# A vision tower on one core: halves of the gate, adjacent logits and moved statistics in the image loop; residual on TensorE in the last part

## What is computed

```python
h = patches(x) @ W.T                               # 768 -> 192
q, k, v = silu(h @ Wq), silu(h @ Wk), silu(h @ Wv) # 12 heads of 16
a = ((q @ k.T) * causal_decay) @ v                 # per head
a = (a * sigmoid(h @ Wg1 @ Wg2)) @ Wo
h = T(h + layernorm(a) * ln_w + ln_b)
# soft mixture: 64 slots, each an expert of its own
xn = rms_norm(h) * norm_w
logits = l2(slots) * scale @ l2(xn).T              # 64 x 196 an image
y = softmax_over_tokens(logits) @ xn               # a slot's input
y = gelu(y @ fc1[s] + b1[s]) @ fc2[s] + b2[s]      # for each slot s
out = T(h + softmax_over_slots(logits).T @ y)
```

## Time and profile before

| | us |
|---|---|
| median of 3 runs (1191.71 to 1193.66) | 1193.31 |
| profiled execution, its own time | 1190.01 |
| its span | 1188.3 |

### The profile page before, as it was taken

How to read it: one execution, slowest core, us unless ns; L and a number is a source line. 1 busy time by engine, 2 the same in 40 slices (tenths; PEclk the granted TensorE clock), 3 DMA queues, 4 the chain that set the end, 5 groups by cost and what they waited for, 6 DMA issues and landing times.

```text
span 1188.3 us, 35236 instructions
## 1 busy us (share of the span) xinstructions
PE 1076.5 (91%) x13008; PEld 837.5 (70%) x13008; DVE 862.8 (73%) x2154; ACT 738.8 (62%) x1711; POOL 628.2 (53%) x967
## 2 busy tenths in 40 slices
PE   7799999999999999999999999999988999996653
PEld 6677788777777777877777778777765655554331
DVE  5878888888888888888888888888872222223996
ACT  6357777777777777777777777777753111110666
POOL 4556666666666665666666666566641000001664
PEclk9999999999999999999999999999999999998555
DMA  4511222111111122111111112211074999995885
GB/s 157 201 52 53 65 88 66 54 54 54 54 54 54 54 69 83 64 54 54 54 54 54 54 54 79 76 61 54 14 306 129 420 423 423 423 424 166 246 257 177
...
## 3 DMA queue, kind: packets, MB, share of 16 engines
...
## 4 chain that ended last, share of the span: by engine, by line
POOL 36%; issue 27%; PE 22%; DVE 10%; ACT 2%; DVEq 1%; DMA 1%; POOLq 1%; ACTq 0%; SPq 0%
POOL xl L440 14%; PE ps L1463 6%; POOL xn L526 5%; PE ps L1482 4%; POOL ra L517 4%; POOL hTl L496 4%; POOL rstd L507 2%; DVE res L1103 2%; POOL invn L500 2%; PE ps L1498 2%; DVE st L1109 2%; PE ps L1489 2%; POOL qd L477 1%; DVE p_sb L947 1%; PE ps L1227 1%
## 5 line engine op out<-in xcount | busy, mean ns | idle before, releaser
L947 DVE TENSOR_TENSOR p_sb<-ps,dec 98x1568 f32<-98x1568 f32 x96 | 171.6, 1788 | 64.2 <-PE ps L1227 64.1
L440 POOL TENSOR_TENSOR xl<-x_sb,xh 128x392 fp32r<-128x392 f32 x186 | 190.2, 1049 | 45.7 <-ACT xh L597 45.7
L496 POOL TENSOR_TENSOR hTl<-hT,hTh 128x392 fp32r<-128x392 f32 x64 | 66.3, 1035 | 146.3 <-ACT hTh L705 98.6
L763 ACT ACTIVATE hg<-ps 128x768 f32<-128x768 f32 x32 | 25.9, 810 | 144.3 <-PE ps L1489 144.3
L883 DVE SCALAR_TENSOR_TENSOR t<-t,rstd,hb 98x192 f32<-98x192 f32 x128 | 93.1, 767 | 15.9 <-POOL rstd L507 15.5
L1095 DVE COPY y2st<-ps 128x192 f32<-128x192 f32 x32 | 11.4, 357 | 120.5 <-PE ps L1463 120.5
L554 POOL CAST pickb<-pick 128x128 fp32r (+1 forms) x32 | 9.4, 293 | 150.4 <-PE ps L1489 150.4
L780 ACT ACTIVATE o_sb<-res,nb,rstd 98x192 f32<-98x192 f32 x128 | 59.6, 536 | 44.6 <-DVE nb L1118 44.0
L1260 PE MATMUL ps<-p_sb,vpad 98*32 98x98 f32 x3072 | 85.7, 252 | 1.5 <-DVE p_sb L947 1.5
L1260 PEld LDWEIGHTS ps<-p_sb,vpad 98*32 98x32 f32 x3072 | 64.7, 110 | 26.7 <-issue 26.7
L1513 PE MATMUL ps<-y2b,cbuf 64*98 64x192 f32 x256 | 49.4, 537 | 37.6 <-POOL y2b L567 37.6
...
## 6 DMA issues: line engine op xcount, KB each, us to landing
...
```

What stands on the lines that cost most here:

```text
L440: pool.tensor_tensor(xl[:, k], x_sb[:, k], xh[:, k].bitcast(F32), ALU.subtract)\
L496: pool.tensor_tensor(hTl[:, k], hT[:, k], hTh[:, k].bitcast(F32), ALU.subtract).then_inc(hTl_rdy[k], 1)
L947: dve.tensor_tensor(dst, src, rate.unsqueeze(2).to_broadcast([T, 4, 2, TOK]), ALU.mult)\
```

## The change

1. **Gate in halves.** `gate(i, 0)` stays; `gate(i, 1)`, with the wait for ScalarE's copies of bank 1, comes after scores part 2.
2. **Logits adjacent.** The four products of the logits of a pair's two images stand together, alternating between the images, before scores part 2.
3. **ScalarE in the step** rounds `x` and copies the logits before the second half of the gate.
4. **VectorE in the step** takes `residual_statistics(i - 1, 1)` after `kts`.
5. **Drain**: half of `xn` and of `hb` is scaled on ScalarE; the squares of pair 31 come before the logits of pair 30 are copied; several steps change place; fewer `idle_products`.
6. **Two-row runs.** `h2` is stored as token rows (two DMAs a pair, 768 B runs); a partition of the last part holds two rows that follow each other, so that `h2r` and the output move in runs of 1536 B. The weights `cbuf` are then read with stride 2.
7. **Last part.** TensorE multiplies `h2r` with the identity into the banks (two products of 384 columns) and adds the four products to it; a signal is sent for each bank. VectorE takes statistics straight from PSUM and adds the bias; GpSimd makes `negm` and `nb3`; ScalarE scales from PSUM; SP issues the stores.

```diff
@@ sync
+                for a in range(2):
+                    sp.dma_start(h2_dram[j, a].rearrange("(k p) d -> p k d", k=2), h2[:, 2 * a:2 * a + 2, :])\
+                        .then_inc(h2_stored, 16)
...
-            sp.wait_ge(sc_mm, 3 * NP)
+            sp.wait_ge(g_mm, 2 * NP)
             load_weights(2, 2)
...
+            def refill(p, n):
+                sp.wait_ge(cmb_mm, 2 * p + 2)
+                load_comb(p + DEEP, n)
+                load_h2(p + DEEP, n)
+
+            def store_out(p, n):
+                sp.wait_ge(o_rdy, 4 * p + 4)
+                sp.dma_start(out_v[p], o_sb[:, n].rearrange("m (a k) d -> m a (k d)", a=2)).then_inc(out_stored[n], 16)
...
+                    refill(p, n)
+                    store_out(p - 2, (n - 2) % DEEP)
@@ gpsimd
+                pool.tensor_tensor(negm[:, n], mv3[:, n, :, 0], expo[0:T, 2], ALU.mult).then_inc(negm_rdy, 1)
                 pool.wait_ge(ve4_rdy, p + 1)
                 pool.tensor_tensor(rstd3[:, n], ve[0:T, n], expo[0:T, 0], ALU.pow).then_inc(rstd3_rdy, 1)
-            def bias(p, n):
-                pool.tensor_tensor(y2b[:, n], y2r[:, p], b2[:, :], ALU.add).then_inc(y2b_rdy, 1)
+                pool.wait_ge(negm_rdy, p + 1)
+                pool.wait_ge(rstd3_rdy, p + 1)
+                pool.tensor_tensor(nb3[:, n], negm[:, n], rstd3[:, n], ALU.mult).then_inc(nb3_rdy, 1)
@@ scalar
                 act.activation(gt[:, 0:PT], ps[:, 0, 0:PT], ACT.Tanh, scale=0.5).then_inc(g_sb, 1)
+                if more:
+                    round_x(i + 1, 1)
+                if d:
+                    logits_kept(i - 2)
                 act.wait_ge(g_mm, 2 * i + 2)
...
-                if more:
-                    round_x(i + 1, 1)
...
+            for t in range(2, 4):
+                act.activation(xn[0:T, t], gn[0:T, t], ACT.Copy, scale=cosc[:, t:t + 1]).then_inc(xn_rdy, 1)
             token_rows(one)
+            squares(last)
             logits_kept(one)
             slot_exponentials(one)
             token_exponentials(one)
-            squares(last)
+            for t in range(2, 4):
+                act.activation(hb[0:T, t], gn[0:T, t], ACT.Copy, scale=cosc[:, t:t + 1]).then_inc(xn_rdy, 1)
...
-                    act.activation(o_sb[:, n, t], res[:, n, t], ACT.Identity,
+                    act.activation(o_sb[:, n, t], ps[0:T, 2 * n + t // 2, (t % 2) * D:(t % 2) * D + D], ACT.Identity,
                                    bias=nb3[:, n, t:t + 1], scale=rstd3[:, n, t:t + 1]).then_inc(o_rdy, 1)
-                act.wait_ge(o_rdy, 4 * p + 4)
-                act.dma_start(out_v[p], o_sb[:, n]).then_inc(out_stored[n], 16)
@@ vector
                     residual(i - 1, 1)
-                    residual_statistics(i - 1, 1)
                 dve.wait_ge(zh_rdy, i + 1)
...
                                   ALU.mult).then_inc(kts_rdy, 1)
+                if c:
+                    residual_statistics(i - 1, 1)
                 decay(i, 1)
...
+            def out_step(p, n, more):
+                for a in range(2):
+                    dve.wait_ge(cmb_mm, 2 * p + a + 1)
+                    for k in range(2):
+                        dve.bn_stats(st3[:, n, 2 * a + k, :], ps[0:T, 2 * n + a, k * D:(k + 1) * D])
+                if more:
+                    bias(p + DEEP, n)
                 dve.drain()
@@ tensor
-            def logits(j, a):
+            def logits(j):
                 pe.wait_ge(tokT_sb, j + 1)
                 for k in range(2):
+                    for a in range(2):
+                        mm = pe.matmul(ps[64 * a:64 * a + 64, 0, 0:TOK], slT[:, k, :],
+                                       tokT[0:G, k, a * TOK:(a + 1) * TOK], start=(k == 0), stop=(k == 1))
...
+            def residual(p, n, w):
+                pe.wait_ge(h2r_loaded[n], 16 * w + 16)
+                for a in range(2):
+                    if not at_start(w):
+                        pe.wait_ge(o_rdy, 4 * (p - DEEP) + 2 * a + 2)
+                    pe.matmul(ps[0:T, 2 * n + a, 0:2 * D], ident[0:T, 0:T],
+                              h2r[:, n, 2 * a:2 * a + 2].rearrange("p t d -> p (t d)"), start=True, stop=False)
+
+            def combined(p, n, w):
+                pe.wait_ge(cbuf_loaded[n], 16 * w + 16)
+                pe.wait_ge(y2b_rdy, p + 1)
+                for a in range(2):
+                    for k in range(2):
+                        mm = pe.matmul(ps[0:T, 2 * n + a, k * D:(k + 1) * D], cbuf[64 * a:64 * a + 64, n, k:TOK:2],
+                                       y2b[64 * a:64 * a + 64, n, :], start=False, stop=(k == 1))
+                    mm.then_inc(cmb_mm, 1)
```

171 lines of the change are left out of this document (76 added, 95 removed).

## The result

The changed kernel takes 1134.64 us (median of 4 runs, 1133.07 to 1139.35), the kernel before 1192.51 us (1189.90 to 1193.66): a ratio of 0.952, with an interval of 0.949 to 0.956. The forecast was 1130, with a range of 1116 to 1156; for the profiled execution it was 1127.1.

What follows compares the result with a forecast made beforehand. One TensorE-VectorE chain bounds the image loop, TensorE the slot loop, VectorE the last part with DMA close behind. 37.7 + 4.5 + 20.7 = 62.9 us off 1190.0 gives 1127.1, forecast as 1130; range 1116 to 1156.

Steps and rivals of the forecast that it cites:

- (a) Statistics: Image loop: moving statistics takes 0.96 us off the way to hb; first p_sb 0.6 earlier, second 0.4.
- (b) Logits: Image loop: all eight logits records together take 0.89 us instead of two times 0.81, saving TensorE 0.8.
- (c) Half gate: Image loop: the second gate product, about 0.2 us, no longer stands ahead of scores part 2.
- (d): Image loop: scores part 2 start at 626.95 instead of 627.79, og at 629.63 instead of 630.87, without waiting for TensorE.
- (e) Hidden work: Image loop: ScalarE's 1.2 us rounding hides before the second gate product is ready; two h2 stores hide too.
- Drain: Behind the slot loop: shorter waits for xn and squares, fewer identity products, smaller edits; 4.5 us, bounds 1 and 7.
- The period: Last part: 2.15 us a pair instead of 2.71, all engines' sums just below it, clock 1.0.
- The start: Last part: statistics of pair 0 start at about 1092.4, with 0.3 us for the add and 0.7 for products.
- The rule on the shared port: Last part: skill says two-input VectorE and GpSimd SBUF instructions exclude each other; forecast: the 98x4 power won't block the bias add.
- Half a step: Rival, image loop: another wait takes over, a step gains only 0.65 us; total 44, 1149 us; chance 0.18.
- Last part at 2.5: Rival: transfers need 2.30 us plus latency, or bias add waits for power; gain 10, 1141 us; chance 0.18.
- Slower, clock at 0.5: Rival, last part: TensorE stays at 1.2 GHz, 4.3 us a pair, 1197 us in all; chance 0.03.

Runs made afterwards that it cites:

- the run with the old loop: Changed kernel with the image loop in the old order (gate whole, logits split, statistics early, ScalarE's old order), two h stores kept; 1177.1 us.
- the second trace: The changed kernel run once more, unaltered, beside other kernels on the same chip; median 1136.5 us, ratio 0.953 to the kernel before.
- the grouped kernel: Changed kernel, VectorE's second y2r wait after four pairs, two pairs' identity products together, then both pairs' combining products; 1136.1 us against 1136.5.

## Why the prediction was right, point by point

**What bounds the kernel.** Right: one chain through TensorE and VectorE in the image loop, where an edit on either engine moves the step, VectorE in the last part. Of the three stages' gains only the image loop's 39.5 us is shown by undoing it; no run puts the addition of `h2r` back on VectorE. Against the 62.9 us off the profiled execution 55.9 were measured (1.8 more in the loop, 1.0 less in the drain, 7.8 less in the last part). That the medians come nearer, 1130 and 1134.6, is luck: the forecast added 3 us because the profiled execution before lay 3.3 below its median, and the one after lay 0.5 below.

**Image loop.** Forecast 1.3 us a step, measured 1.42; 37.7 us in all, measured 39.5. *(a) Statistics*: the sum gave 0.6 for the first `p_sb` and 0.4 for the second. Undone alone they cost 0.75, so the term was small by a quarter to a half, unless that cost holds some of the 0.30 that another edit is needed for too. *(b) Logits*: 0.8 forecast, 0.78 measured. *(c) Half gate*: 0.2 and 0.19. *(d)* The waits: ahead of the third `p_sb` 1.1 was forecast and 0.93 measured, ahead of `og` none and none. The place was partly off. I had the split logits hold up scores part 2. They did in the kernel before (second `p_sb` done at 625.46 + 1.79 = 627.25, scores at 627.79), but with the other two edits in place they no longer do: the run with the logits split has scores part 2 1.87 us after the start of the second `p_sb`, as the changed kernel has (574.62 - 572.75), and there it is the half behind them that `og` waits for. *(e) Hidden work*: right. The rounding ends before the half gate is there (ScalarE waits 0.83 for it), and the two stores of `h2` cost nothing, as the run with the old loop shows (26.95).

**Drain.** 4.5 forecast, 3.5 measured between two traces that each had a low clock for a while (0.97 over the stretch); the second trace without that has 48.5 us, 5.1 less than before, but no trace of the kernel before is without it. It was within its bounds of 1 to 7, by other waits than named. For `xn` TensorE waits 1.4 instead of 2.98, but for `Es` 1.2 instead of 0.8. VectorE's wait for the squares is gone, but 1.3 us for GpSimd's `ra` stands in its place. The largest piece is a wait of TensorE that the sum didn't name. The kernel before had it, in the changed one it is gone:

```profile
PE ps L1324 <- DVE DT L928: 2.0, 1, 2.0
```

Which of the reordered steps took it away, no run tells.

**Last part.** 20.7 forecast, 12.9 measured. This is the part that was mis-sized, in two terms.

*The period*, 2.15 forecast, 2.30 measured: the term is TensorE's sum. The identity products took 1.46 instead of 1.3, the combining ones 0.84 instead of 0.75. The rows that I priced them from held nearly that. The four products in two rounds of two took 1.51, and two identity products have a record of 1.53; I took 1.3 out of the 1.51 and gave no reason. The old combining products took 1.61 at clock 0.50, half of which is 0.8, not 0.75. As read, the rows give 2.3. What I had left off is the cost of changing between kinds: products among their own kind do cost 1.29 and 0.73, 2.02 in all, the 2.0 to 2.1 of the sum, and the changes cost the other 0.28. From the first statistics of the first pair to those of the last it was 70.9 us (1124.0 - 1053.1), where 66.7 had been forecast: 4.2 us. The steady 0.15 in all 31 would be 4.6; the first pairs add what the clock cost, and take off that they come at VectorE's pace.

*The start*: forecast 6.2 us after the last `y2st`, measured 9.9, 3.7 us, because the wait for the second load of `y2r` moved with the bias into VectorE's stream, ahead of the statistics; before, it stood in GpSimd's stream, where nothing waited behind it for the first four pairs but their scales. The diff of the kernels shows it, and the working passed over it. It cost 3.1 us and, through TensorE's idle 5.9 us, part of a clock.

*The rest of it held*: VectorE works 19.52 / 25 x 2.30 = 1.80 us a pair, a little over the 1.67 of the sum (1.9 with its idle time); ScalarE 1.74 (at most 1.85), clock 1.00, DMA 0.95 x 2.30 = 2.19 (between 1.94 and 2.30), and 8.4 us from the first statistics of the last pair to the end (8.5 forecast).

**The rule on the shared port.** The bias adds took their 0.34 us, so nothing blocked VectorE. The start of the last part puts it to the test that the prediction had in mind, a power under a bias add, and then comes a steady pair:

```profile
1055.38 1.01 POOL L582 TENSOR_TENSOR rstd<-ve,expo 98x4 f32<-98x4 f32 x1
...
1055.95 0.34 DVE L1113 TENSOR_TENSOR y2b<-y2r,b 128x192 f32<-128x192 f32 x1
...
1084.87 1.01 POOL L582 TENSOR_TENSOR rstd<-ve,expo 98x4 f32<-98x4 f32 x1
...
1085.98 0.34 DVE L1113 TENSOR_TENSOR y2b<-y2r,b 128x192 f32<-128x192 f32 x1
1086.02 0.36 POOL L585 TENSOR_TENSOR nb<-negm,rstd 98x4 f32<-98x4 f32 x1
...
1127.15 0.20 POOL L585 TENSOR_TENSOR nb<-negm,rstd 98x4 f32<-98x4 f32 x1
```

At 1055.95 the add begins 0.57 us into the power, and neither takes longer; so it is in three pairs of this trace and in fifteen of the grouped kernel's. So this reason for 2.5 us a pair is out by a row, not only by argument, and what the Trainium skill ("SBUF — State Buffer", Who interferes with whom) says, that the later of the two waits until the first has ended, doesn't hold for this power. In the steady pair they don't meet: the power ends at 1085.88, a tenth before the add begins. It is `nb` that runs beside the add, and there it takes 0.36; in the last pairs, which have no bias add beside them, it takes 0.20. It starts 0.04 after the add and ends 0.06 after it, so here it is GpSimd's product that waits. That fits the Trainium skill's rule, at 0.16 us a pair on an engine with room. But where `nb` begins first by its record (0.20 before the add in one pair of the grouped kernel) it also ends 0.06 after the add, and takes 0.60; so the start of a record doesn't tell who comes first.

**The rivals.** *Half a step*: no, 1.42. *Last part at 2.5*: no, and neither of its two reasons; but its neighbourhood was right, since the transfers come to 2.29 when TensorE no longer sets the pace. *Slower, clock at 0.5*: no; but the clock did fall at the start, for one to three pairs of 3.4 to 4.35 us, at about the price per pair that the rival gave (4.3); the second trace of the changed kernel has 4.35 and 4.33.
